# Attention maxima on quarters of the array, in 64-query tiles; score products issued in pairs of heads

## The chip, the cores and the metric

One NeuronCore of one Trainium2 chip runs the whole program. The metric is device time in microseconds. Three runs of the kernel before took 1016.52, 1017.29 and 1020.27 us (median 1017.29). A difference of under 0.5% can't be told from none.

## The reference

Two layers, each a mixer gated by a feed-forward branch, on x of shape (4, 1024, 128). The change touches only the first mixer, causal softmax attention with 16 heads of depth 8:

```python
scores = jnp.einsum('bhnd,bhmd->bhnm', Q, K) / jnp.sqrt(jnp.float32(D_K))
scores = jnp.where(causal[None, None], scores, -jnp.inf)
attn = jax.nn.softmax(scores, axis=-1)
head = jnp.einsum('bhnm,bhmd->bhnd', attn, V)
```

Around it stand a layernorm, rotary embedding, a gelu feed-forward, and in the second layer a retention mixer and a top-2 mixture of eight experts.

## The kernel before, in words

The program runs in stages: projections and first feed-forward, `attention`, the work between the layers, retention with routing, experts. Everything below is in `attention`. Each engine's instruction stream is written out in order; engines meet through semaphores, and no planner reorders anything.

The work is cut into 16 groups (`NQ`), one for each batch and each four heads. Q and K of a group lie in SBUF as `q_groups` and `k_groups`: 64 partitions hold one head (split into bf16 parts, plus two rows that take the negated maximum), so two heads fill the 128 partitions and `hq // 2` selects the pair. A score product of one head uses one 64-row half of TensorE.

Per group there are two streams of 40 items each.

- **Maxima** (`for_maximum`, L877): the row maximum of every query. A unit is 128 queries by up to 512 keys of one head, or of two heads of the same half when the width is at most 256. TensorE writes it to one of four banks (`RING` = 4); on the diagonal two masking matmuls (`causal`, L897) add -1e30 above it. VectorE reduces the bank to one number for each row (`tensor_reduce`, L766). Before unit n is written, `max_read` must say that unit n-4 has been reduced. After the 40 units VectorE combines the two key halves (L769), GpSimd splits the maxima into bf16 parts (L815 to L821), TensorE turns them over (`turn_over`, L874), VectorE copies them out (L756), and SyncE places them by two DMAs in the augmentation rows of Q (`place`, L677).
- **Products** (`for_products`, L906): scores again, now transposed and with the maximum subtracted. A step is 128 keys by up to 512 queries of one head (or two). It goes to one of three banks (`BANKS` = 3); masking matmuls stand at L928. ScalarE takes the exponential into `probs` (L854). Before step n is written, `exp_done` must say that step n-3 is through ScalarE. Five steps behind, `products` (L959) multiplies the probabilities with V in fp32, for four heads at once on tiles of 128 rows by 32 columns. ScalarE copies the finished halves out (`keep`, L841), once after step 4 and once after step 16 of a group, in line with its exponentials.

The loop over group x runs the products of x and, beside them, the maxima of x+1 (units 16 to 39) and x+2 (units 0 to 15). `side_by_side` (L936) issues one product step and one maximum unit on opposite halves of the array, then the masks of both; `turn_over` comes at step 28. `packs`, `units` and `steps` (L595 to L607) are ordered so that both items of a pair have the same width. A prologue does the maxima of group 0 and a part of group 1 before any product.

Of the kernel before, what the change touches and what calls it, by code (L numbers as in the profile page):

```python
# [20 lines left out]
BF16 = mybir.dt.bfloat16  # L21
# [27 lines left out]
ROW = D + 2  # L49
BUFS = 3  # L50
MASKED = -1.0e30
MAGNITUDE = 0x7FFFFFFF
LN_EPS, RMS_EPS, TOP_EPS = 1e-5, 1e-6, 1e-9

# [39 lines left out]
class Groups:  # L94


    def __init__(self, m):
        self.q, self.k = m.sb("q_groups", [P, QUADS, 2, S], BF16), m.sb("k_groups", [P, QUADS, 2, S], BF16)
        self.zeroed = m.sem("groups_zeroed")
        self.loaded = [m.sem(f"groups_loaded{s}") for s in range(QUADS)]  # L100
        self.masks = [m.sb(n, [P, 2, P], BF16) for n in ("chooseB", "hideB", "hide_laterB")]
        self.masks_loaded = m.sem("masks_loaded")

    def load_masks(self, sp, A):
# [484 lines left out]
def attention(nc, A, groups, second, kept_until):  # L589

    NQ = B * QUADS
    slots = [(0, 0), (0, 1), (0, 3), (0, 2), (1, 0), (1, 2), (1, 4), (1, 5), (1, 3), (1, 7), (1, 6), (1, 1)]
    tiles = [(2, 0), (4, 0), (0, 0), (1, 0), (5, 0), (3, 0), (6, 1), (4, 1), (5, 1), (6, 0), (7, 0), (7, 1)]

    def packs(w):  # L595

        return [(0, 2), (1, 3)] if 2 * w <= HALF else [(hq,) for hq in range(4)]

    def max_width(t, c):
        return min(HALF, P * (t + 1) - HALF * c)  # L600

    def slot_width(j):
        c, jt = slots[j]
        return HALF * (c + 1) - max(HALF * c, P * jt)

    units = [(tuple(hq ^ 1 for hq in heads), t, c) for t, c in tiles for heads in packs(max_width(t, c))]
    steps = [(j, heads) for j in range(len(slots)) for heads in packs(slot_width(j))]  # L607
    assert [max_width(t, c) for _, t, c in units[16:] + units[:16]] == [slot_width(j) for j, _ in steps]
# [17 lines left out]
    def offset(heads, hq, w):  # L626

        return heads.index(hq) * w
# [6 lines left out]
    with Space(nc) as m:  # L635
# [6 lines left out]


        q, k, in_loaded = groups.q, groups.k, groups.loaded
        mx, mx2 = m.sb("mxB", [P, 2, 2, 2, NT]), m.sb("mx2B", [P, 2, 2, 2, NT // 2])
# [12 lines left out]
        LOADS, PLACED, STORED, SOURCES = 16 * 5, 16 * 2, HEAD_STORES, 16 * 4  # L658
# [5 lines left out]
        with nc.Block() as block:  # L664
            @block.sync
            def _(sp):
# [73 lines left out]
            def _(dve):  # L740
# [4 lines left out]
                for n, (x, g) in enumerate(order):  # L745
                    if n == AHEAD:
                        nc.vector.memset(empty[:, :, 0:D + 1], 0.0).then_inc(emptied, 1)
                        nc.vector.memset(empty[:, :, D + 1], float(2 * N)).then_inc(emptied, 1)
                    par = x % 2
                    if (x, g) == (SCALED, None):  # L750
                        reciprocals(0)
                    dve.wait_ge(max_done, n + 1)
                    if g is None:
                        if x >= 2:
                            dve.wait_ge(neg_placed[par], PLACED * (x // 2))
                        nc.vector.tensor_copy(neg[:, par, :], mxb[n % RING][0:64, 0:P]).then_inc(max_read, 1)  # L756
                        continue
                    heads, t, c = units[g]
                    w = max_width(t, c)
                    table, col = (mx, t) if c == 0 else (mx2, t - 4)  # L760
                    if len(heads) == 1:
                        dst, src = table[:, par, heads[0] % 2, heads[0] // 2, col:col + 1], mxb[n % RING][:, 0:w]
                    else:
                        dst = table[:, par, heads[0] % 2, :, col]
                        src = mxb[n % RING][:, 0:2 * w].rearrange("p (a w) -> p a w", w=w)
                    nc.vector.tensor_reduce(dst, src, AX.X, ALU.max).then_inc(max_read, 1)  # L766
                    if g == UNITS - 1:
                        dve.wait_ge(max_read, n + 1)
                        nc.vector.tensor_tensor(mx[:, par, :, :, 4:8], mx[:, par, :, :, 4:8], mx2[:, par, :, :, :],  # L769
                                                ALU.max).then_inc(combined, 1)  # L770

                dve.wait_ge(g2["in_loaded"], SOURCES)
# [28 lines left out]
            def _(pool):  # L801
# [10 lines left out]
                def split_maxima(x):  # L812
                    par, upper, lower = x % 2, parts[:, x % 2, 0, :], parts[:, x % 2, 1, :]
                    pool.wait_ge(combined, x + 1)
                    nc.gpsimd.tensor_scalar(lower, mx[:, par, :, :, :].rearrange("p a b t -> p (a b t)"), -1.0, None,  # L815
                                            ALU.mult).then_inc(split, 1)
# [50 lines left out]
            def _(pe):  # L867
# [9 lines left out]
                def for_maximum(x, g):  # L877

                    n = place_of[x, g]
                    s = x % QUADS  # L880
                    heads, t, c = units[g]
                    w = max_width(t, c)
# [4 lines left out]
                    bank = mxb[n % RING]  # L887

                    def score(i):
                        hq = heads[i]  # L890
                        r, to = hq % 2, offset(heads, hq, w)
                        ins = nc.tensor.matmul(bank[:, to:to + w], q[half[r], s, hq // 2, t * P:t * P + P],  # L892
                                               k[half[r], s, hq // 2, HALF * c:HALF * c + w], start=True, stop=(c < t // 4))
                        if c < t // 4:
                            ins.then_inc(max_done, 1)

                    def causal(i, part):  # L897
                        r, to = heads[i] % 2, offset(heads, heads[i], w) + w
                        ins = nc.tensor.matmul(bank[:, to - P + ROWS * part:to], choose[half[r], part, :],  # L899
                                               hide[half[r], part, ROWS * part:P], start=False, stop=(part == 1))  # L900
                        if part == 1 and i == len(heads) - 1:
                            ins.then_inc(max_done, 1)

                    return len(heads), score, None if c < t // 4 else causal

                def for_products(x, e):  # L906

# [79 lines left out]
                for x, g in prologue:  # L987
                    if g is None:
                        turn_over(x)
                    else:  # L990
                        side_by_side(for_maximum(x, g))
                waiting = []
                for x in range(NQ):
                    todo = stream(x)
                    pe.wait_ge(neg_placed[x % 2], PLACED * (x // 2 + 1))
                    for e, (j, heads) in enumerate(steps):
                        both = [for_products(x, e)]
                        if todo and todo[0][1] is None:
                            turn_over(todo.pop(0)[0])
                        if todo:  # L1000
                            both.append(for_maximum(*todo.pop(0)))
                        side_by_side(*both)
                        if e == last_step[j]:
                            waiting.append((x, j))
                        if waiting and due(*waiting[0]) <= UNITS * x + e:
# [1215 lines left out]
def constants():  # L2221
# [22 lines left out]
    hide = np.where(p[None, None, :] > row, MASKED, 0.0)  # L2244
# [72 lines left out]
```

## Time and profile before

| | us |
|---|---|
| Median of three runs | 1017.29 |
| Span of the profiled execution (first to last instruction) | 1008.0 |
| Outside the span, against the median | 9.3 |
| Maxima prologue, then the attention loop | about 117 to 148, then 148 to 540 |
| VectorE busy in a steady stretch of the loop, 215.0 to 482.7 | 254.24 of 267.70 |
| TensorE busy in it (ends are modelled) | 252.06 |
| ScalarE busy in it | 226.13 |

The profile is of one execution. "PE" is TensorE's matmuls, "PEld" its weight loads, "DVE" VectorE, "ACT" ScalarE, "POOL" GpSimd, "SP" SyncE, and a "q" behind a name is that engine's queue, as it issues DMAs. Of the tile in `64*128` the first number is rows of the array, the second columns. Durations of TensorE, VectorE and ScalarE instructions overlap with their successors, so a rate is read from starts, not from durations: of a merged line of n equal instructions it is (length less one duration) over n-1.

### The profile page before, as it was taken

Reading aid. Unit: us, or ns where it says so; the run is one execution under the profiler, and the core shown is the slowest. Engines: PE = TensorE matmul, PEld = TensorE weight load, DVE = VectorE, ACT = ScalarE, POOL = GpSimd, SP = SyncE. Lnnn points to the kernel's source line nnn. Section 1 sums busy time; section 2 is a strip of 40 time slices with the busy share of each in tenths; the row PEclk is TensorE's granted clock in tenths of the full one; section 3 lists DMA queues with packets and bytes.
Section 4 is the critical chain, followed back from the end, with each engine's and each line's share of the span. In section 5 each row is a group of like instructions: output and inputs, shape, how many; then the busy total and the mean of one; then the engine's idle time right before and its main releaser. Section 6 shows DMA issues by size and latency. Waiting matters only on the chain. (4 is left out here: it accounts for less than half of the span.)

```text
span 1008.0 us, 25094 instructions
## 1 busy us (share of the span) xinstructions
PE 874.2 (87%) x9373; PEld 464.7 (46%) x9374; DVE 816.2 (81%) x1699; ACT 725.7 (72%) x1493; POOL 289.1 (29%) x331
## 2 busy tenths in 40 slices
PE   4999899899999999999898898778999999979960
PEld 3666543334333333333344666533444444458850
DVE  6665499899999999999923766589999999928895
ACT  2666408788888888888784454478999999948851
POOL 4865311111111000000003656500344443005560
PEclk9999859999999999999999888768999999989995
DMA  5579851644445353330004899695354643546637
GB/s 167 223 267 331 280 133 42 205 101 105 110 98 125 89 123 84 68 69 14 13 24 127 277 317 301 226 241 101 67 118 94 114 89 54 136 142 189 206 119 252
DMA packets 121560, 147.20 MB, mean 146 GB/s; under 512 B 19213, under 2 KB 81242, under 8 KB 120800
## 3 DMA queue, kind: packets, MB, share of 16 engines
q1 hardware_dynamic: 116064, 133.74, 48.0%
q0 software_dynamic: 5376, 11.85, 4.1%
q8 instruction: 76, 1.25, 0.5%
q14 instruction: 44, 0.36, 0.1%
HBM read 77.63 MB, written 69.54 MB: 146 GB/s over the span
## 5 line engine op out<-in xcount | busy, mean ns | idle before, releaser
L854 ACT ACTIVATE probsB<-psB 128x512 f32<-128x512 f32 (+2 forms) x640 | 310.0, 566 | 87.1 <-PE psB L928 61.5
L766 DVE TENSOR_REDUCE mxB<-psB 128x1 f32<-128x512 f32 (+2 forms) x448 | 256.9, 642 | 11.1 <-PE psB L892 8.3
L921 PE MATMUL psB<-q_groups,k_groups 64*128 64x512 bf16 (+3 forms) x768 | 205.8, 330 | 16.6 <-DVE mxB L766 8.3
L892 PE MATMUL psB<-k_groups,q_groups 64*128 64x512 bf16 (+3 forms) x768 | 217.0, 344 | 2.8 <-PEq L293 1.7
L959 PE MATMUL psB<-probsB,vB 128*32 128x512 f32 (+3 forms) x1536 | 164.5, 500 | 0.7 <-ACT probsB L854 0.5
L1725 ACT ACTIVATE psD<-psD 128x896 f32<-128x896 f32 (+2 forms) x192 | 153.4, 799 | 12.9 <-PE psD L1779 12.7
L921 PEld LDWEIGHTS psB<-q_groups,k_groups 64*128 64x128 bf16 x768 | 67.5, 94 | 161.2 <-ACT probsB L854 140.3
L1656 DVE TENSOR_REDUCE sumsD<-psD 128x1 f32<-128x128 f32 (+3 forms) x256 | 113.2, 481 | 11.8 <-PE psD L1802 9.4
L899 PE MATMUL psB<-hideB,chooseB 64*128 64x128 bf16 (+1 forms) x1024 | 115.1, 210 | 0.0
L1779 PE MATMUL psD<-k_groups,q_groups 64*128 64x512 bf16 (+3 forms) x384 | 104.4, 343 | 12.3 <-ACT psD L1725 5.6
L766 DVE TENSOR_REDUCE mx2B<-psB 128x1 f32<-128x384 f32 (+2 forms) x192 | 104.4, 594 | 8.5 <-PE psB L899 6.9
L928 PE MATMUL psB<-hide_laterB,chooseB 64*128 64x64 bf16 (+1 forms) x1024 | 109.7, 205 | 0.0
L815 POOL TENSOR_SCALAR partsB<-mxB 128x32 f32<-128x32 f32 x16 | 4.6, 290 | 346.7 <-DVE mxB L769 346.7
L928 PEld LDWEIGHTS psB<-hide_laterB,chooseB 64*128 64x128 bf16 x1024 | 88.6, 95 | 19.8 <-issue 1.4
L899 PEld LDWEIGHTS psB<-hideB,chooseB 64*128 64x128 bf16 x1024 | 92.2, 98 | 9.9 <-issue 3.9
L1711 POOL DMA_INDIRECT slot_x<-xD,indexR x64 | 64.4, 1006 | 77.8 <-DVE sumsD L1656 39.5
L1667 DVE TENSOR_TENSOR keptD<-psD,causalD 128x512 f32<-128x512 f32 x128 | 82.5, 680 | 0.3 <-PE psD L1798 0.2
L892 PEld LDWEIGHTS psB<-k_groups,q_groups 64*128 64x128 bf16 x768 | 69.0, 95 | 13.4 <-DVE mxB L766 9.2
L1960 POOL DMA_INDIRECT back<-zE,toE x40 | 44.3, 1107 | 86.8 <-DVE zE L2147 76.7
L1779 PEld LDWEIGHTS psD<-k_groups,q_groups 64*128 64x128 bf16 x384 | 29.8, 96 | 80.8 <-ACT psD L1725 47.4
L1802 PE MATMUL psD<-k_groups,q_groups 64*128 64x128 bf16 (+3 forms) x256 | 64.8, 314 | 0.9 <-DVE keptD L1667 0.9
L1798 PE MATMUL psD<-q_groups,k_groups 64*128 64x128 bf16 x512 | 49.0, 225 | 6.8 <-DVE sumsD L1656 6.2
(227 smaller groups left out, 1504.5 us busy)
## 6 DMA issues: line engine op xcount, KB each, us to landing
v<-vaugA SPq DMA_DIRECT2D x4, 2048.0 KB, 8.9
vB<-v SPq DMA_DIRECT2D x16, 512.0 KB
q_groups<-q SPq DMA_DIRECT2D x32, 200.0 KB
k_groups<-k SPq DMA_DIRECT2D x32, 200.0 KB
q_groups<-q SPq DMA_DIRECT2D x32, 192.0 KB
k_groups<-k SPq DMA_DIRECT2D x32, 192.0 KB
back<-emptyB POOLq DMA_DIRECT2D x16, 256.0 KB, 3.8
o<-outB SPq DMA_DIRECT2D x128, 32.0 KB, 1.8
```

The source lines that it names most:

```text
L766: nc.vector.tensor_reduce(dst, src, AX.X, ALU.max).then_inc(max_read, 1)
L854: nc.scalar.activation(probs[:, n % DEEP, 0:w], st[n % BANKS][:, 0:w], ACT.Exp, scale=DH ** -0.5).then_inc(exp_done, 1)
L892: ins = nc.tensor.matmul(bank[:, to:to + w], q[half[r], s, hq // 2, t * P:t * P + P], k[half[r], s, hq // 2, HALF * c:HALF * c + w], start ...
L899: ins = nc.tensor.matmul(bank[:, to - P + ROWS * part:to], choose[half[r], part, :], hide[half[r], part, ROWS * part:P], start=False, stop ...
L921: ins = nc.tensor.matmul(bank[:, to:to + w], k[half[r], s, hq // 2, jt * P:jt * P + P], q[half[r], s, hq // 2, i0:i0 + w], start=True, sto ...
L928: ins = nc.tensor.matmul(bank[:, to:to + ROWS * (part + 1)], choose[half[r], part, :], hide_later[half[r], part, 0:ROWS * (part + 1)], sta ...
L959: ins = nc.tensor.matmul(pv[VW * hq:VW * hq + VW, HALF - w:HALF], v[:, s, jt, VW * hq:VW * hq + VW], probs[:, (UNITS * x + at) % DEEP, to: ...
L1656: ins = V.tensor_reduce(sums[:, s, unit:unit + 1], src[:, at:at + P * t], AX.X, ALU.add, apply_absolute_value=True)
L1667: V.tensor_tensor(dst[:, :, :, half, :], piece_bank[n % PIECE_RING].rearrange("p (t a i) -> p t a i", t=2, a=2), causal[:, None, None, :]. ...
L1725: nc.scalar.activation(src, src, ACT.Abs, accum_out=sums[:, s, unit:unit + 1]).then_inc(score_read, 1)
L1779: ins = nc.tensor.matmul(score[n % SCORE_RING][:, cols], q[r, s, hq // 2, P * t:P * t + P], k[r, s, hq // 2, cols], start=True, stop=True)
L1802: ins = nc.tensor.matmul(bank[:, at:at + P * t], q[r, s, hq // 2, P * t:P * t + P], k[r, s, hq // 2, 0:P * t], start=True, stop=True)
```

## The change

- Queries of the maxima go in tiles of 64 (`ROW_TILE`). A unit is now (f, t, c): the two heads 2f and 2f+1, query tile t of 16, key half c (None: tile t with keys of half 0 and tile t+8 with half 1, side by side in one bank). Each head writes 64 partitions of the bank, so each score matmul uses a quarter of the array (64 rows by 64 columns), and the units f = 0 and f = 1 use the four different quarters. Widths end at the diagonal in steps of 64. There are still 40 units.
- One masking matmul of 64 columns for each head and diagonal tile, instead of two of 64 and 128 columns.
- The loop issues two product steps side by side (on the two halves), then two maxima units together (`maxima`), every second step, instead of one product step beside one maxima unit each step. `turn_over` stands between the two.
- The maxima lie in another order in `neg`, so `place` issues eight DMAs of one destination row for each group instead of two.

```diff
-    tiles = [(2, 0), (4, 0), (0, 0), (1, 0), (5, 0), (3, 0), (6, 1), (4, 1), (5, 1), (6, 0), (7, 0), (7, 1)]
+    kinds = [(5, 0), (13, 1), (14, 0), (2, None), (1, None), (15, 0), (7, 0), (15, 1), (8, 0), (9, 0), (4, 0), (12, 1), (0, None),
+             (3, None), (10, 0), (6, 0), (11, 0), (14, 1), (12, 0), (13, 0)]
+    def max_width(f, t, c):
+        return min(HALF, first_row(f, t) + ROW_TILE - HALF * c)
+    def heads_of(f, r):
+        return [(2 * f + r, 64 * (r ^ f))] if ROW_TILE == 64 else [(2 * a + r, 64 * (r ^ f) + ROW_TILE * a) for a in range(2)]
+    units = [(f, t, c) for t, c in kinds for f in range(2)]
...
                     for part in range(2):
-                        sp.dma_start(q[AUG + part:AUG + part + ROWS + 1:ROWS, x % QUADS, :, :],
-                                     neg[32 * part:32 * part + 32, x % 2, :]).then_inc(neg_placed[x % 2], 16)
+                        for f in range(2):
+                            for r in range(2):
...
+                                    sp.dma_start(dst, neg[src, x % 2, at:at + ROW_TILE]).then_inc(neg_placed[x % 2], 16)
...
                     def score(i):
+                        ti, ci = segments[i]
+                        w = max_width(f, ti, ci)
+                        last = first_row(f, ti) // HALF > ci
+                        for r in range(2):
+                            for hq, at in heads_of(f, r):
+                                ins = nc.tensor.matmul(bank[at:at + ROW_TILE, w * i:w * i + w],
+                                                       q[half[r], s, hq // 2, first_row(f, ti):first_row(f, ti) + ROW_TILE],
+                                                       k[half[r], s, hq // 2, HALF * ci:HALF * ci + w], start=True, stop=last)
...
+                    def causal(i):
+                        ti, ci = segments[i]
+                        to = max_width(f, ti, ci) * (i + 1)
+                        for r in range(2):
+                            at = 64 * (r ^ f)
+                            ins = nc.tensor.matmul(bank[at:at + 64, to - ROW_TILE:to], choose[half[r], 0, 0:64], hide[half[r], :],
+                                                   start=False, stop=True)
...
+                def maxima(*both):
+                    for i in range(both[0][0]):
+                        for n, score, _ in both:
+                            if i < n:
+                                score(i)
+                        for n, _, causal in both:
+                            if causal and i < n:
+                                causal(i)
...
                     for e, (j, heads) in enumerate(steps):
-                        both = [for_products(x, e)]
-                        if todo and todo[0][1] is None:
-                            turn_over(todo.pop(0)[0])
-                        if todo:
-                            both.append(for_maximum(*todo.pop(0)))
-                        side_by_side(*both)
+                        if e % 2 == 0:
+                            side_by_side(for_products(x, e), for_products(x, e + 1))
+                            if todo and todo[0][1] is None:
+                                turn_over(todo.pop(0)[0])
+                            if todo:
+                                maxima(*[for_maximum(*todo.pop(0)) for _ in range(2)])
```

## Rows read from the trace of the kernel before

**Rows 1.** The page, part 1: busy us (share of the span) x instructions.
```profile
PE 874.2 (87%) x9373; PEld 464.7 (46%) x9374; DVE 816.2 (81%) x1699; ACT 725.7 (72%) x1493; POOL 289.1 (29%) x331
```

**Rows 2.** Busy time by stretch: length, then PE, PEld, DVE, ACT, POOL; granted clock.
```profile
115.00:142.00 27.00, 23.67 (x133) 11.01 (x131) 24.66 (x48) 3.83 (x4) 1.24 (x7) 0.56 0.72 183
...
215.00:482.70 267.70, 252.06 (x3615) 102.68 (x3615) 254.24 (x474) 226.13 (x471) 21.36 (x59) 1.00 0.38 87
...
507.00:535.00 28.00, 26.01 (x269) 11.91 (x265) 6.91 (x29) 23.23 (x51) 1.87 (x2) 1.00 0.32 79
```

**Rows 3.** Waits, 215.0 to 482.7: us in total, times, longest.
```profile
PEld psB L921 <- ACT probsB L854: 101.3, 158, 0.9
...
DVE mxB L766 <- PE psB L892: 6.9, 11, 0.6
```

**Rows 4.** VectorE in order of time: start, length of the merged run, idle before.
```profile
140.60 1.94 DVE L766 TENSOR_REDUCE mxB<-psB 128x1 f32<-128x384 f32 x4
...
262.70 0.27 DVE L756 CAST negB<-psB 64x128 bf16<-64x128 f32 x1
...
264.25 8.53 DVE L766 TENSOR_REDUCE mxB<-psB 128x1 f32<-128x512 f32 x15 [0.63 <-PE psB L892]
...
277.02 4.86 DVE L766 TENSOR_REDUCE mxB<-psB 128x1 f32<-128x512 f32 x8
...
286.55 0.27 DVE L756 CAST negB<-psB 64x128 bf16<-64x128 f32 x1
```

**Rows 5.** TensorE's matmuls in order of time, five short stretches.
```profile
264.24 0.38 PE L892 MATMUL psB<-k_groups,q_groups 64*128 64x512 bf16 x1
264.55 0.85 PE L959 MATMUL psB<-probsB,vB 128*32 128x384 f32 x8
265.33 0.23 PE L921 MATMUL psB<-q_groups,k_groups 64*128 64x128 bf16 x1
...
265.48 0.22 PE L921 MATMUL psB<-q_groups,k_groups 64*128 64x128 bf16 x1
...
270.18 0.39 PE L921 MATMUL psB<-q_groups,k_groups 64*128 64x512 bf16 x1
...
270.49 0.38 PE L892 MATMUL psB<-k_groups,q_groups 64*128 64x512 bf16 x1
...
271.64 0.19 PE L899 MATMUL psB<-hideB,chooseB 64*128 64x64 bf16 x1
271.75 1.06 PE L959 MATMUL psB<-probsB,vB 128*32 128x512 f32 x8
272.75 0.33 PE L921 MATMUL psB<-q_groups,k_groups 64*128 64x384 bf16 x1
...
273.01 0.32 PE L892 MATMUL psB<-k_groups,q_groups 64*128 64x384 bf16 x1
...
301.48 0.43 PE L959 MATMUL psB<-probsB,vB 128*32 128x128 f32 x8
...
301.84 0.39 PE L921 MATMUL psB<-q_groups,k_groups 64*128 64x512 bf16 x1
```

**Rows 6.** One loop of TensorE, ScalarE and weight load, in order of time.
```profile
267.53 0.60 ACT L854 ACTIVATE probsB<-psB 128x512 f32<-128x512 f32 x1
...
268.02 0.39 PE L921 MATMUL psB<-q_groups,k_groups 64*128 64x512 bf16 x1
...
268.51 2.06 ACT L854 ACTIVATE probsB<-psB 128x512 f32<-128x512 f32 x4 [0.37 <-PE psB L921]
...
270.18 0.09 PEld L921 LDWEIGHTS psB<-q_groups,k_groups 64*128 64x128 bf16 x1 [0.41 <-ACT probsB L854]
```

**Rows 7.** Placing the maxima; last row: DMA issues, with us to landing.
```profile
197.66 0.39 PE L921 MATMUL psB<-q_groups,k_groups 64*128 64x512 bf16 x1 [1.65 <-DMA q_groups<-negB]
...
286.85 1.08 SPq L677 DMA_DIRECT2D q_groups<-negB  x2
...
o<-outB SPq DMA_DIRECT2D x116, 32.0 KB, 2.1
```

More of the change, by code:

```diff
@@ L51 @@
 MASKED = -1.0e30
+ROW_TILE = 64
 MAGNITUDE = 0x7FFFFFFF
@@ L100, in __init__ @@
         self.loaded = [m.sem(f"groups_loaded{s}") for s in range(QUADS)]
-        self.masks = [m.sb(n, [P, 2, P], BF16) for n in ("chooseB", "hideB", "hide_laterB")]
+        self.masks = [m.sb(n, shape, BF16) for n, shape in (("chooseB", [P, 2, P]), ("hideB", [P, ROW_TILE]), ("hide_laterB", [P, 2, P]))]
         self.masks_loaded = m.sem("masks_loaded")
@@ L592, in attention @@
     slots = [(0, 0), (0, 1), (0, 3), (0, 2), (1, 0), (1, 2), (1, 4), (1, 5), (1, 3), (1, 7), (1, 6), (1, 1)]
-    tiles = [(2, 0), (4, 0), (0, 0), (1, 0), (5, 0), (3, 0), (6, 1), (4, 1), (5, 1), (6, 0), (7, 0), (7, 1)]
[L595 to L600, printed above, removed]
+    kinds = [(5, 0), (13, 1), (14, 0), (2, None), (1, None), (15, 0), (7, 0), (15, 1), (8, 0), (9, 0), (4, 0), (12, 1), (0, None),
+             (3, None), (10, 0), (6, 0), (11, 0), (14, 1), (12, 0), (13, 0)]
     def slot_width(j):
@@ L604, in slot_width, with packs, row_tile, first_row @@
         return HALF * (c + 1) - max(HALF * c, P * jt)
-    units = [(tuple(hq ^ 1 for hq in heads), t, c) for t, c in tiles for heads in packs(max_width(t, c))]
+    def packs(w):
+        return [(0, 2), (1, 3)] if 2 * w <= HALF else [(hq,) for hq in range(4)]
+    def row_tile(f, t):
+        return 16 * f + t if ROW_TILE == 64 else 2 * t + f
+    def first_row(f, t):
+        return ROW_TILE * (t if ROW_TILE == 64 else 2 * t + f)
+    def max_width(f, t, c):
+        return min(HALF, first_row(f, t) + ROW_TILE - HALF * c)
+    def heads_of(f, r):
+        return [(2 * f + r, 64 * (r ^ f))] if ROW_TILE == 64 else [(2 * a + r, 64 * (r ^ f) + ROW_TILE * a) for a in range(2)]
+    def parts_of(f, t, c):
+        return [(t, 0), (t + 8, 1)] if c is None else [(t, c)]
+    units = [(f, t, c) for t, c in kinds for f in range(2)]
     steps = [(j, heads) for j in range(len(slots)) for heads in packs(slot_width(j))]
-    assert [max_width(t, c) for _, t, c in units[16:] + units[:16]] == [slot_width(j) for j, _ in steps]
+    assert len(units) == len(steps)
     UNITS, SLOTS_B = len(units), len(slots)
@@ L644, in attention @@
         q, k, in_loaded = groups.q, groups.k, groups.loaded
-        mx, mx2 = m.sb("mxB", [P, 2, 2, 2, NT]), m.sb("mx2B", [P, 2, 2, 2, NT // 2])
+        mx = m.sb("mxB", [P, 2, 2, 2, 16])
         neg = m.sb("negB", [64, 2, P], BF16)
@@ L657, in attention @@
         neg_placed = [m.sem(f"neg_placedB{p}") for p in range(2)]
-        LOADS, PLACED, STORED, SOURCES = 16 * 5, 16 * 2, HEAD_STORES, 16 * 4
+        LOADS, PLACED, STORED, SOURCES = 16 * 5, 16 * 8 * (64 // ROW_TILE), HEAD_STORES, 16 * 4
         SCALED, PROJECT_AT, TURN_AT = QUADS + 3, 2, 20
@@ L676, in place @@
                     for part in range(2):
-                        sp.dma_start(q[AUG + part:AUG + part + ROWS + 1:ROWS, x % QUADS, :, :],
-                                     neg[32 * part:32 * part + 32, x % 2, :]).then_inc(neg_placed[x % 2], 16)
+                        for f in range(2):
+                            for r in range(2):
+                                row, src = ROWS * r + AUG + part, slice(32 * part + 16 * f, 32 * part + 16 * f + 16)
+                                for hq, at in heads_of(f, r):
+                                    dst = q[row:row + 1, x % QUADS, hq // 2, :]
+                                    dst = dst.rearrange("p (t i) -> p t i", i=ROW_TILE) if ROW_TILE == 64 else (
+                                        dst.rearrange("p (t f i) -> p f t i", f=2, i=ROW_TILE)[:, f])
+                                    sp.dma_start(dst, neg[src, x % 2, at:at + ROW_TILE]).then_inc(neg_placed[x % 2], 16)
                 def store(x, c):
@@ L757, in _ @@
                         continue
[L758 to L762, printed above, removed]
-                    else:
-                        dst = table[:, par, heads[0] % 2, :, col]
-                        src = mxb[n % RING][:, 0:2 * w].rearrange("p (a w) -> p a w", w=w)
+                    f, t, c = units[g]
+                    w = max_width(f, t, c or 0)
+                    if c is None:
+                        dst, src = mx[:, par, :, f, t], mxb[n % RING][:, 0:2 * w].rearrange("p (a w) -> p a w", w=w)
+                    else:
+                        dst, src = mx[:, par, c, f, t - 8 * c:t - 8 * c + 1], mxb[n % RING][:, 0:w]
                     nc.vector.tensor_reduce(dst, src, AX.X, ALU.max).then_inc(max_read, 1)
@@ L814, in split_maxima @@
                     pool.wait_ge(combined, x + 1)
-                    nc.gpsimd.tensor_scalar(lower, mx[:, par, :, :, :].rearrange("p a b t -> p (a b t)"), -1.0, None,
+                    nc.gpsimd.tensor_scalar(lower, mx[:, par, 0, :, :].rearrange("p f t -> p (f t)"), -1.0, None,
                                             ALU.mult).then_inc(split, 1)
@@ L880, in for_maximum @@
                     s = x % QUADS
-                    heads, t, c = units[g]
-                    w = max_width(t, c)
+                    f, t, c = units[g]
                     if n >= RING:
@@ L886, in for_maximum @@
                         pe.wait_ge(in_loaded[s], LOADS * (x // QUADS + 1))
-                    bank = mxb[n % RING]
+                    bank, segments = mxb[n % RING], parts_of(f, t, c)
                     def score(i):
[L890 to L894, printed above, removed]
-                            ins.then_inc(max_done, 1)
@@ L897, in causal @@
[L897 to L901, printed above, removed]
+                        ti, ci = segments[i]
+                        w = max_width(f, ti, ci)
@@ new lines, in score @@
+                        last = first_row(f, ti) // HALF > ci
+                        for r in range(2):
+                            for hq, at in heads_of(f, r):
+                                ins = nc.tensor.matmul(bank[at:at + ROW_TILE, w * i:w * i + w],
+                                                       q[half[r], s, hq // 2, first_row(f, ti):first_row(f, ti) + ROW_TILE],
+                                                       k[half[r], s, hq // 2, HALF * ci:HALF * ci + w], start=True, stop=last)
@@ new lines, in score @@
+                        if last:
+                            ins.then_inc(max_done, 1)
+                    def causal(i):
[5 more added lines that the diff above has]
+                                                   start=False, stop=True)
+                        if i == len(segments) - 1:
@@ L902, in causal @@
                             ins.then_inc(max_done, 1)
-                    return len(heads), score, None if c < t // 4 else causal
+                    on_diagonal = first_row(f, t) // HALF == (c or 0)
+                    return len(segments), score, causal if on_diagonal else None
                 def for_products(x, e):
@@ L990, in _ @@
                     else:
-                        side_by_side(for_maximum(x, g))
+                        maxima(for_maximum(x, g))
                 waiting = []
@@ L2243, in constants @@
     choose = np.where(p[None, None, :] == row, 1.0, 0.0)
-    hide = np.where(p[None, None, :] > row, MASKED, 0.0)
+    hide = np.where(np.arange(ROW_TILE)[None, :] > p[:, None] % ROW_TILE, MASKED, 0.0)
     hide_later = np.where(p[None, None, :] < row, MASKED, 0.0)
```

2 lines of the change are left out of this document (1 added, 1 removed).

## The prediction

> **What bounds the kernel now.** I read the page's busy shares first [rows 1]: TensorE is busy 87% of the span, VectorE 81%, ScalarE 72%, which says little, as the stages have different limits. So I took busy time by stretch next. In the steady attention loop [rows 2] VectorE is busy 254.24 of 267.70 us (95%), TensorE 252.06 with modelled ends, ScalarE 226.13. The waits of that stretch [rows 3] decide between the first two: VectorE's longest account with TensorE is 6.9 us, 11 times, while TensorE's loads for a product wait for ScalarE 158 times. VectorE in order of time [rows 4] shows reductions back to back and one 0.63 us hole behind each turn-over. One group takes 286.55 - 262.70 = 23.85 us, cast to cast. VectorE is the bound; TensorE follows it through the ring of four banks.
>
> VectorE's rate, from starts [rows 4]: 512 columns (4.86 - 0.68) / 7 = 0.598 us, 384 columns (1.94 - 0.55) / 3 = 0.464. That is 1.05 ns a column and 0.06 us an instruction. The 40 units of a group hold 18,432 columns: 19.3 + 2.5 us, with cast and combine 22.1, and 1.7 us idle make the 23.85.
>
> TensorE's prices [rows 5] (w columns at the granted 1.00, 2.4 GHz, stream in w / 2.4 ns: 0.213 us for 512):
> - a score pair with its masks: 512 wide 270.49 - 270.18 = 0.31; 384 wide 273.01 - 272.75 = 0.26; packed 128, 265.48 - 265.33 = 0.15 for each of two; packed 256 by the same slope 0.20. Masks alone are about 0.09.
> - a change of tile shape: from the last score of 512 at 264.24 to the probabilities-times-V matmuls (PV below) at 264.55 is 0.31, less 0.213 streaming: 0.09. From a 64-column mask at 271.64 to 271.75 is 0.11, less 0.03: 0.09 again.
> - PV with the change back: 512 wide 272.75 - 271.75 = 1.00, 384 wide 0.78, 128 wide 0.36, 256 between them 0.57. Less 0.09 each: 0.91, 0.69, 0.27, 0.48.
>
> A group has 18,432 columns of score pairs (7.68), 32 masked pairs (2.7), 12 PV (six of 512, two each of 384, 256, 128: 8.3), 24 changes of shape (2.2) and the turn-over (0.3): 21.2 us of TensorE, under VectorE's 22.1.
>
> **What the change does to each engine.**
>
> *VectorE.* Widths end at multiples of 64: the 20 kinds sum to 8,704, twice that is 17,408 columns, still 40 reductions. Saved: 1,024 x 1.05 ns = 1.07 us a group. This is a gain only if VectorE stays the bound.
>
> *TensorE, work.* Product scores pairwise: 4 masked pairs of 512 (0.31), 8 unmasked (0.21), 4 masked of 384 (0.26), 2 packed of 128 (twice 0.14) and 2 of 256 (twice 0.205) are 5.4 us a group. Maxima: if four quarters stream at once, 8,704 columns / 2.4 = 3.6 us, with 16 rounds of 64-column masks, each about 0.06 with its load (between the 0.03 of streaming and the 0.09 of today's masks): 4.6. The bounds are 4.6 and, if only two stream at once, 8.2. I take 4.6, since PV already runs four matmuls on four column strips together: two passes of 512 columns for four heads, eight matmuls, end in 1.06 us [rows 5]. PV 8.3, turn-over 0.3. Scores are thus 10.0 instead of 10.4: pairing saves almost nothing, because before the pair was product and maximum.
>
> *TensorE, changes of shape.* The order is now products (64*128), maxima (64*64), products again, or PV (128*32) between. That is 2 x 20 + 12 = 52 changes a group instead of 24. The trace shows no change between 64*128 and 64*64; the bounds are 0 and the 0.09 of the nearest rows (rows 5). I take 0.09, for both changes that can be read have it: 4.7 us. Sum of the work: 5.4 + 4.6 + 8.3 + 4.7 + 0.3 = 23.3 us, above VectorE's new 21.0.
> The Trainium skill, TensorEngine Tiling (Array Packing), section Key Properties, says that changing the tiling mode drains the TensorEngine, while changing only the tile does not. The trace agrees for the changes it has, 0.09 us each; no row shows whether 64*64 beside 64*128 counts as another mode. By the rule the forecast stands, without it the first rival below.
>
> *TensorE, the new wait.* There are three score banks. A pair (e, e+1) may be written only when the exponential of e-2 is done, which is the *first* of the pair before. So from one pair to the next lies at least: score to ScalarE's start 268.51 - 268.02 = 0.49 [rows 6], one exponential 0.60, wake-up about 0.07 (four exponentials take 2.06, so they start 0.487 apart, and the third ends at 268.51 + 0.97 + 0.60 = 270.08; the load that waits for it starts at 270.18; 0.07 is an estimate below this 0.10). That is 1.15 us for 512 unmasked, 1.24 masked, 1.09 for 384 masked, 0.99 and 1.34 for the packed ones of 128 and 256. Before, the wait reached three single steps back and bound nothing. Behind the waiting instruction stand the maxima units, so VectorE is starved by it too, and PV, since TensorE runs in order.
> PV stands in every second pair of a single-head slot. The pair with PV costs its work: 512 masked 0.31 + 0.09 + 0.21 + 0.09 + 0.91 + 0.09 = 1.70. The one without has 0.7 of work but may not follow sooner than 1.24. Two pairs: 2.94 (unmasked 2.75), where VectorE needs 4 x 0.598 = 2.39.
>
> *The group.* Pair by pair, the larger of work and wait (pair number = step / 2): 1.27, 1.24, 1.63, 1.81, 0.99, 1.34, 1.39, 1.15, then 2.94 for pairs 8 and 9, 1.70, 1.24, 1.66, 1.09, 1.91 (turn-over), 1.45, 0.99, 1.34, 1.67, 1.15. Pair 3 holds 0.18 because its PV waits for ScalarE's copy of the group before; pairs 8 and 9 because the exponential of step 18 stands behind the copy after step 16, which waits for PV of pair 8. Sum 27.96: 23.3 of work and 4.7 of waits. Against 23.85: +4.1 us a group, for the 14 groups that run both streams: +57.5.
>
> *The rest.* The last but one group loses its maxima half way (27 us before; estimate +1). The last has products alone [rows 2]: pairs now share the array, but the wait of about 1.15 a pair makes 24 us of 20 pairs, and it took about 26 with the output projection in it: 0, bounds -3 and +2. The prologue is VectorE's (24.66 busy of 27): 1,280 columns less, -1.3.
>
> *Placing.* Eight DMAs at 0.54 us to issue [rows 7] are 4.3 us where two took 1.1. The first goes out 0.30 behind the cast (286.55 to 286.85), the last 3.8 later, and it lands between 2.1 (the nearest store) and some 4 us after that: 6 to 8 us from the cast. The pairs behind the cast now last about 8, so it hides mostly, but not in the prologue nor in the group at 197.66, which already waits 1.65 for it: +3 in all, bounds +1 and +12 (0.8 a group).
>
> **Sum.** 57.5 + 1 + 0 - 1.3 + 3 = +60. The span goes from 1008.0 to 1068, and with the 9.3 us around it from 1017.3 to 1077.
>
> **The rivals.**
> - *No cost between 64*128 and 64*64.* 0.09 less in the ten pairs that are bound by work: 0.85 x 14 = 12 less, 1065. For: only the column split changes. Against: both changes seen cost the same.
> - *Quarters in one bank take turns.* The two heads of a unit lie in different row halves but in one bank. Then the maxima stream twice as long: +2.4 us a group in the work-bound pairs, +34, 1111. For: today's two halves always write to different banks, so the trace shows nothing that excludes it. Against: the partitions differ. The Trainium skill, same page, section Gotcha 1: PSUM Pressure, says that different row tiles can't access the same PSUM bank at once; no row here shows it.
> - *The other side: VectorE stays the bound.* If two pairs take TensorE under 2.39 us, VectorE goes on back to back and only its saving counts: 1.07 x 14 + 1.3 = 16 less, 1001. It is one mechanism, the in-order chain of scores, maxima and PV hiding in VectorE's ring of four, and it decides at 2.39. For: VectorE has two units in hand while TensorE does PV. Against: PV with its changes (1.0), two shared score rounds (0.5) and one wait (1.15) already exceed it with free changes of shape.
> - *It evens out.* Waits overlap with work so far that a group takes its 23.9 us; 1017.
>
> **Chances.** Forecast 0.63 (1077, own range 1062 to 1092), free change of shape 0.12 (1065), turns in a bank 0.12 (1111), VectorE stays 0.08 (1001), even 0.05. The range of 1045 to 1112 leaves out the last two and tails. Faster by over 0.5% 0.08, within 0.5% (what a measurement here can't tell from none) 0.05, slower 0.87.
>
> **What would show it.** In the loop: cast to cast about 28 us; VectorE busy near 21 of 28 with waits for TensorE in every second pair; the load of each product pair waiting for ScalarE; 0.09 beyond streaming from the last product score to the first maximum; four maxima matmuls starting within 0.03. Cast to cast under 23.85, or VectorE above 90% busy, would make the prediction wrong, and first of all the bank wait.

## The result, and the profile after

The changed kernel takes 1097.72 us (median of 4 runs, 1095.68 to 1098.78) against 1016.9 (4 runs) before: ratio 1.0784, interval 1.0755 to 1.0813. I had forecast 1077. The profiled execution spans 1097.0 us, from the first instruction to the last. Every run lies about 1.8 us above the span of its core, so the 9.3 us that I put outside the span before were mostly one quick execution: its 1008.0 us of span stand for about 1010 of time. The ratios below are of fast executions alone; the one slow execution, of e4 at 1896 us, is left out.

The page, part 1, and busy time by stretch (length, then PE, PEld, DVE, ACT, POOL), the steady loop and the last group, against [rows 1, 2]. L949 are now the score matmuls of the products, L956 their masks, L915 and L926 those of the maxima, L997 the products with V, L875 the exponentials, L787 the reductions.

```profile
PE 900.6 (82%) x10142; PEld 465.3 (42%) x10142; DVE 814.7 (74%) x1699; ACT 737.9 (67%) x1493; POOL 289.3 (26%) x331
```
```profile
215.00:475.00 260.00, 218.26 (x3303) 83.39 (x3306) 203.51 (x378) 187.98 (x377) 20.25 (x51) 1.00 0.36 82
...
591.00:619.00 28.00, 20.52 (x234) 8.92 (x234) 6.91 (x29) 21.16 (x43) 1.87 (x2) 1.00 0.40 100
```

No engine is near full in the loop: VectorE fell from 95% to 78%, TensorE is at 84% and ScalarE at 72%. VectorE in order of time has the casts of two groups [rows 4] 28.95 us apart, and between them ten holes of 0.38 to 0.97 us, two of which are here:

```profile
288.53 0.28 DVE L779 CAST negB<-psB 64x128 bf16<-64x128 f32 x1
...
311.80 1.29 DVE L787 TENSOR_REDUCE mxB<-psB 128x1 f32<-128x512 f32 x2 [0.78 <-PE psB L915]
313.54 1.29 DVE L787 TENSOR_REDUCE mxB<-psB 128x1 f32<-128x512 f32 x2 [0.46 <-PE psB L915]
...
317.48 0.28 DVE L779 CAST negB<-psB 64x128 bf16<-64x128 f32 x1
```

The waits of 220.0 to 500.0 (total us, times, longest), against [rows 3]:

```profile
PEld psB L949 <- ACT probsB L875: 127.5, 183, 1.4
ACT probsB L875 <- PE psB L956: 44.1, 105, 1.1
...
DVE mxB L787 <- PE psB L926: 39.3, 65, 1.0
ACT probsB L875 <- PE psB L949: 20.4, 40, 0.8
DVE mxB L787 <- PE psB L915: 18.2, 32, 0.8
```

VectorE waits for TensorE 57.5 us in 97 waits; ScalarE and TensorE wait for each other. A pair is steps 2p and 2p + 1 of a group. TensorE in order of time through pairs 11 and 12 shows why:

```profile
342.03 0.39 PE L949 MATMUL psB<-q_groups,k_groups 64*128 64x512 bf16 x2
342.25 0.25 PE L956 MATMUL psB<-hide_laterB,chooseB 64*128 64x64 bf16 x4
342.43 0.41 PE L915 MATMUL psB<-k_groups,q_groups 64*64 64x512 bf16 x4
343.34 0.34 PE L949 MATMUL psB<-q_groups,k_groups 64*128 64x384 bf16 x2 [0.49 <-ACT probsB L875]
...
343.69 0.36 PE L915 MATMUL psB<-k_groups,q_groups 64*64 64x384 bf16 x4
343.88 0.20 PE L926 MATMUL psB<-hideB,chooseB 64*64 64x64 bf16 x4
344.01 1.06 PE L997 MATMUL psB<-probsB,vB 128*32 128x512 f32 x8
345.00 0.34 PE L949 MATMUL psB<-q_groups,k_groups 64*128 64x384 bf16 x2
```

And ScalarE beside it, with the idle time before each run:

```profile
342.60 1.08 ACT L875 ACTIVATE probsB<-psB 128x512 f32<-128x512 f32 x2 [0.67 <-PE psB L956]
343.84 0.87 ACT L875 ACTIVATE probsB<-psB 128x384 f32<-128x384 f32 x2 [0.16 <-PE psB L956]
```

ScalarE starts on the pair of 342.03 at 342.60, its first exponential ends 0.60 later, and the next pair starts at 343.34: 1.31 us, in which TensorE has 0.75 of work (what the same pair takes in e1 below). Then everything behind that wait, products, maxima and PV (the block of probabilities times V), takes 345.00 - 343.34 = 1.66. Four steps cost 2.98 us (2.97 by the rounded starts). Before they cost 2.52, by the starts of the same steps in TensorE's order of time, pair 11 at 306.25, pair 12 at 307.15 and the next at 308.76:

```profile
306.25 0.38 PE L921 MATMUL psB<-q_groups,k_groups 64*128 64x512 bf16 x1
...
307.15 0.33 PE L921 MATMUL psB<-q_groups,k_groups 64*128 64x384 bf16 x1
...
307.50 1.06 PE L959 MATMUL psB<-probsB,vB 128*32 128x512 f32 x8
...
308.76 0.32 PE L921 MATMUL psB<-q_groups,k_groups 64*128 64x384 bf16 x1
```

Where 81 us went, by starts of the first exponential: 14 full groups +71.6, the last but one +4.8, the last +3.0; the first product starts 2.7 later (150.7 against 148.0). That is 82. The two profiled spans differ by 89.0; the other 7 lie behind the attention, in work that the change doesn't touch, and that took between 467 and 481 us in the fourteen profiles.

### The profile page after: what moved, and what is told of

It reads as the page before. It is cut to its first block and busy times, and to the rows that moved or that the text cites. A ratio compares the mean times of both kernels' runs of the same rounds, so it can differ in the third digit from the quotient of the medians.

```text
span 1097.0 us, 26753 instructions
## 1 busy us (share of the span) xinstructions
PE 900.6 (82%) x10142; PEld 465.3 (42%) x10142; DVE 814.7 (74%) x1699; ACT 737.9 (67%) x1493; POOL 289.3 (26%) x331
## 5 line engine op out<-in xcount | busy, mean ns | idle before, releaser
L787 DVE TENSOR_REDUCE mxB<-psB 128x1 f32<-128x512 f32 (+7 forms) x640 | 354.8, 605 | 96.8 <-PE psB L926 63.8
L875 ACT ACTIVATE probsB<-psB 128x512 f32<-128x512 f32 (+2 forms) x640 | 320.4, 554 | 141.8 <-PE psB L956 104.0
L949 PE MATMUL psB<-q_groups,k_groups 64*128 64x512 bf16 (+3 forms) x768 | 125.4, 332 | 77.6 <-ACT probsB L875 70.4
L997 PE MATMUL psB<-probsB,vB 128*32 128x512 f32 (+3 forms) x1536 | 166.4, 506 | 3.0 <-ACT outB L862 2.6
L915 PE MATMUL psB<-k_groups,q_groups 64*64 64x512 bf16 (+7 forms) x1536 | 136.7, 346 | 5.4 <-DVE mxB L787 2.6
L949 PEld LDWEIGHTS psB<-q_groups,k_groups 64*128 64x128 bf16 x768 | 42.3, 93 | 226.3 <-ACT probsB L875 212.8
L915 PEld LDWEIGHTS psB<-k_groups,q_groups 64*64 64x64 bf16 x1536 | 46.7, 106 | 58.4 <-DVE mxB L787 33.4
L956 PE MATMUL psB<-hide_laterB,chooseB 64*128 64x64 bf16 (+1 forms) x1024 | 60.6, 204 | 0.0
L956 PEld LDWEIGHTS psB<-hide_laterB,chooseB 64*128 64x128 bf16 x1024 | 49.7, 95 | 11.4 <-issue 0.7
L926 PE MATMUL psB<-hideB,chooseB 64*64 64x64 bf16 x1024 | 50.5, 195 | 0.0
L2076 ACT ACTIVATE hTE<-psE,b1E 128x320 f32<-128x320 f32 x64 | 33.3, 527 | 24.1 <-PE psE L2035 23.5
L997 PEld LDWEIGHTS psB<-probsB,vB 128*32 128x32 f32 x1536 | 30.8, 108 | 41.4 <-issue 35.4
```

Of the source, the lines that this page charges most:

```text
L875: nc.scalar.activation(probs[:, n % DEEP, 0:w], st[n % BANKS][:, 0:w], ACT.Exp, scale=DH ** -0.5).then_inc(exp_done, 1)
L915: ins = nc.tensor.matmul(bank[at:at + ROW_TILE, w * i:w * i + w], q[half[r], s, hq // 2, first_row(f, ti):first_row(f, ti) + ROW_TILE], k[ ...
L949: ins = nc.tensor.matmul(bank[:, to:to + w], k[half[r], s, hq // 2, jt * P:jt * P + P], q[half[r], s, hq // 2, i0:i0 + w], start=True, sto ...
L956: ins = nc.tensor.matmul(bank[:, to:to + ROWS * (part + 1)], choose[half[r], part, :], hide_later[half[r], part, 0:ROWS * (part + 1)], sta ...
L997: ins = nc.tensor.matmul(pv[VW * hq:VW * hq + VW, HALF - w:HALF], v[:, s, jt, VW * hq:VW * hq + VW], probs[:, (UNITS * x + at) % DEEP, to: ...
```

## The experiments

All twelve ran beside the kernel before; ratios are to it, as it ran beside them (its medians were 1012.9 us for e1 to e4, 1018.1 for e5 to e8 and 1017.2 for e9 to e12). "Group" is the steady time of a group. Pairs 11 and 12 are start to start of the product pairs, the second with a PV block of 512 columns.

| kernel | ratio (interval) | group | pair 11 | pair 12 | both |
|---|---|---|---|---|---|
| before | 1 | 23.85 | 0.91 | 1.61 | 2.52 |
| changed | 1.078 (1.076 to 1.081) | 28.94 | 1.31 | 1.67 | 2.98 |
| e1 waits split | 1.062 (1.057 to 1.068) | 27.94 | 0.75 | 2.13 | 2.88 |
| e2 old maxima, in pairs | 1.065 (1.060 to 1.071) | 28.20 | 1.31 | 1.60 | 2.91 |
| e3 e2, waits split | 1.048 (1.041 to 1.054) | 27.19 | 0.61 | 2.20 | 2.81 |
| e4 four score banks | 1.063 (1.055 to 1.070) | 28.36 | 0.75 | 2.25 | 3.00 |
| e5 maxima first | 1.062 (1.057 to 1.067) | 27.84 | 1.31 | 1.35 | 2.66 |
| e6 e5, waits split | 1.047 (1.043 to 1.050) | 26.81 | 0.94 | 1.63 | 2.57 |
| e7 single products | 1.051 (1.047 to 1.055) | 27.07 | 1.21 | 1.67 | 2.88 |
| e8 before, four score banks | 1.013 (1.009 to 1.017) | 24.75 | 1.02 | 1.61 | 2.63 |
| e9 half exponentials | 1.053 (1.049 to 1.056) | 26.90 | 1.10 | 1.67 | 2.76 |
| e10 before, half exponentials | 0.994 (0.991 to 0.996) | 23.35 | 0.69 | 1.61 | 2.30 |

**The loop through ScalarE, shortened (e9, e10).** This is the most direct test. From group 3 on each exponential covers half the columns of its step, so part of the softmax is left out; TensorE's and VectorE's instructions stay the same.

```diff
-                        w = slot_width(j) * len(heads)
+                        w = slot_width(j) * len(heads) // (2 if x > 2 else 1)
```

> The changed kernel with the exponentials of groups 3 to 15 on half the columns of a step (the other half of the probabilities keeps older values): part of the softmax is left out, TensorE's and VectorE's instructions are the same. ScalarE takes about 0.33 us for a step instead of 0.60. Theory (the loop score, exponential, freed bank sets the distance of two pairs): every pair without a long PV block comes 0.27 us sooner, down to its work, and pairs 3 and 9 lose their copy chain: 2.7 us less a group, 26.3 (25.8 to 26.8), ratio to the kernel before 1.047 (1.04 to 1.055). Rival (TensorE's matmuls and changes of shape fill the time): a group within 0.3 us of 28.9.

TensorE and ScalarE of e9 in order of time, at the same pair:

```profile
334.80 0.39 PE L949 MATMUL psB<-q_groups,k_groups 64*128 64x512 bf16 x2
335.20 0.41 PE L915 MATMUL psB<-k_groups,q_groups 64*64 64x512 bf16 x4
335.90 0.34 PE L949 MATMUL psB<-q_groups,k_groups 64*128 64x384 bf16 x2 [0.28 <-ACT probsB L875]
```
```profile
335.37 0.66 ACT L875 ACTIVATE probsB<-psB 128x256 f32<-128x256 f32 x2 [1.10 <-PE psB L956]
```

The distance fell from 1.31 to 1.10, as the exponential fell from 0.60 to 0.38; it is still 0.57 from matmul to ScalarE's start. Pairs 0, 2, 10, 12, 14, 15 and 18, which are bound by work, did not change by 0.01 us; pairs 1, 4, 5, 7, 11, 13, 16, 17 and 19 each lost 0.11 to 0.21, and pair 9 lost 0.42. The group is 26.90, just above the 25.8 to 26.8 that was forecast (the saving is 0.22 a pair, not 0.27, and pair 3 kept its chain through the copy); the ratio, 1.053, is inside its range. The rival is out: the same matmuls and changes of shape took 2.0 us less.

> The same omission in the kernel before. Theory: VectorE bounds it, with ScalarE's loop just under it, so a group goes from 23.85 to no less than 23.0, ratio 0.99 (0.985 to 1.0). Rival (the kernel before is held by the same loop): 22 us or less a group, ratio under 0.98.

23.35: the theory held. The kernel before has a little of the same loop, since it gained 0.5 us (pair 11 went from 0.91 to 0.69).

**Each wait just before its own matmul (e1).**

```diff
-                    if n >= BANKS:
-                        pe.wait_ge(exp_done, n - BANKS + 1)
                     bank = st[n % BANKS]
                     def score(i):
+                        if i == 0 and n >= BANKS:
+                            pe.wait_ge(exp_done, n - BANKS + 1)
```

> The changed kernel, but each of the two product steps of a pair waits for its own score bank just before its first matmul, instead of both waits before either matmul. The first of a pair then goes out one exponential earlier and ScalarE has it in hand. My theory (the bank wait is what holds the pairs without a probabilities-times-V block at about 1.3 us): those pairs drop to their work, a group from 28.94 to 24.0 to 25.0 us, the whole to about 1030 us (1020 to 1042). Rival (TensorE's work, with its changes of tile shape and its quarters, is the cost): a group stays above 28 us, the whole within 1% of 1098 us.

A miss for both: 27.94. TensorE of e1 in order of time, and its weight loads with the wait inside the pair:

```profile
336.19 0.39 PE L949 MATMUL psB<-q_groups,k_groups 64*128 64x512 bf16 x2
...
336.94 0.81 PE L949 MATMUL psB<-q_groups,k_groups 64*128 64x384 bf16 x2
...
337.76 0.36 PE L915 MATMUL psB<-k_groups,q_groups 64*64 64x384 bf16 x4
...
338.07 1.06 PE L997 MATMUL psB<-probsB,vB 128*32 128x512 f32 x8
339.07 0.34 PE L949 MATMUL psB<-q_groups,k_groups 64*128 64x384 bf16 x2
```
```profile
337.41 0.09 PEld L949 LDWEIGHTS psB<-q_groups,k_groups 64*128 64x128 bf16 x1 [0.38 <-ACT probsB L875]
```

The pair without PV indeed fell to its work, 0.75. But the fourth product step since PV (337.41) still waits for the exponential of the first (from 336.19: 1.22 us), and the maxima and PV stand behind it: 1.66 to the next pair. Three banks allow three steps ahead, whatever the form of the wait. So the price of four steps is first product to freed bank, plus all that is issued in order behind that wait. My forecast had taken the wait for the pair's own.

**The old maxima in the new order (e2), and with split waits (e3).**

```diff
+                        if e % 2 == 0:
+                            side_by_side(for_products(x, e), for_products(x, e + 1))
...
+                            if todo:
+                                side_by_side(*[for_maximum(*todo.pop(0)) for _ in range(2)])
```

> The kernel before (maxima of 128 queries on 64x128 tiles, two placing DMAs), with only the order changed: two product steps side by side, then two maxima units side by side. My theory (bank wait first, change of tile shape second): a group 27.8 to 28.4 us, 0.1 us less in the ten pairs bound by work, the whole about 1084 us (1076 to 1092). Rival (the 28 added changes of shape are the main cost): 28.94 - 2.7 = 26.2 us, about 1057 us. Rival (the quarters are the main cost): back to 23.9 us, about 1017 us.

28.20, as forecast: with no quarters, no added changes of shape and two placing DMAs, the order alone costs 4.35 of the 5.1 us. Both rivals are out. TensorE of e2 in order of time at pair 11:

```profile
334.71 0.39 PE L921 MATMUL psB<-q_groups,k_groups 64*128 64x512 bf16 x2
334.94 0.25 PE L928 MATMUL psB<-hide_laterB,chooseB 64*128 64x64 bf16 x4
335.03 0.38 PE L892 MATMUL psB<-k_groups,q_groups 64*128 64x512 bf16 x2
335.24 0.25 PE L899 MATMUL psB<-hideB,chooseB 64*128 64x128 bf16 x4
336.02 0.34 PE L921 MATMUL psB<-q_groups,k_groups 64*128 64x384 bf16 x2 [0.53 <-ACT probsB L854]
```

> As the one before, with the waits of a product pair taken one at a time. TensorE's work is then 21.4 us a group by the sum of the prediction, below VectorE's 22.1. My theory: VectorE is the bound again, a group 23.3 to 24.6 us, the whole about 1017 us (1010 to 1030). Rival (the order in pairs costs in itself, whatever the waits): above 26 us, 1050 us or more.

27.19; my theory missed and the rival held. The reason is the one seen in e1, as far as the pairs tell (0.61 and 2.20): the pair of maxima stands behind the wait in the stream, where in the kernel before one of its two units goes out beside the product.

**Only the place of the maxima (e5, e6).**

```diff
+                            first = bool(waiting) and due(*waiting[0]) <= UNITS * x + e + 1
+                            if not first:
+                                side_by_side(for_products(x, e), for_products(x, e + 1))
...
+                            if first:
+                                side_by_side(for_products(x, e), for_products(x, e + 1))
```

> The changed kernel with one thing in another order: in a pair of steps that ends with a probabilities-times-V block, the two maxima units are issued ahead of the two product steps, so they lie in the time in which TensorE waits for ScalarE. Nothing is added or taken away but some 7 changes of shape. Theory as the first runs leave it: two pairs cost first product to freed bank (1.26 us) plus all that stands behind the wait (products, maxima, PV: 1.7). With the maxima ahead, 1.4 stands behind: 0.3 us less in seven or eight pairs, a group 26.3 to 27.0 us, the ratio to the kernel before 1.045 (1.035 to 1.055). Rival (TensorE's work is the bound, waits only fill it): only the changes of shape count, 0.7 us a group, 28.2 us, ratio 1.068 or more.

27.84, ratio 1.062: a miss for both, less than the theory's gain and more than the rival's. TensorE of e5 in order of time:

```profile
334.02 0.39 PE L949 MATMUL psB<-q_groups,k_groups 64*128 64x512 bf16 x2
334.42 0.57 PE L915 MATMUL psB<-k_groups,q_groups 64*64 64x512 bf16 x8
335.33 0.34 PE L949 MATMUL psB<-q_groups,k_groups 64*128 64x384 bf16 x2 [0.30 <-ACT probsB L875]
335.68 1.07 PE L997 MATMUL psB<-probsB,vB 128*32 128x512 f32 x8
336.68 0.34 PE L949 MATMUL psB<-q_groups,k_groups 64*128 64x384 bf16 x2
...
338.16 0.41 PE L915 MATMUL psB<-k_groups,q_groups 64*64 64x512 bf16 x4 [0.28 <-DVE mxB L787]
```

Where it applies it does what it should: the maxima go into the waiting time, 1.31 + 1.35 = 2.66 for 2.98. But only pairs 3, 9, 10, 12, 14 and 15 gain (0.22 to 0.34 each). The others with a PV block don't: pair 2, for one, is followed by a pair that has a block too, whose maxima now lie ahead of it and so in the place of pair 2's own (1.64 us, as in the change). And pair 13 takes 0.67 longer, since behind the turn-over two pairs of maxima follow each other and the second waits for VectorE (338.16).

> Both edits: maxima ahead of the products before a PV block, and each product's wait just before its own matmul. Theory: the gains of the two add (1.0 for the wait, 2.3 for the order), a group 25.3 to 26.2 us, ratio 1.03 (1.02 to 1.045). Rival (both act on the same idle time): no better than the order alone, 26.3 us or more.

26.81, ratio 1.047: the theory's 25.3 to 26.2 missed, because the order alone gained only 1.1. The rival's number holds, but not the rival, which had both acting on the same idle time and so no gain over the order alone: 1.00 for the wait and 1.10 for the order are 2.10, and 2.13 was measured. It has the shortest group of the versions with quarters, and is far from the kernel before.

**The quarters alone (e7).**

```diff
-                            side_by_side(for_products(x, e), for_products(x, e + 1))
+                            side_by_side(for_products(x, e))
...
+                        else:
+                            side_by_side(for_products(x, e))
```

> The quarters alone: two maxima units together every second step as in the change, but the product steps go out one at a time, one ahead of the maxima and one behind, each with the wait of the kernel before (three steps back). Theory: a masked slot costs 0.31, 0.1, 0.21, 0.1, 0.31 shared with the next step, 0.1, 0.21, 0.1, then 0.31 and PV 1.1: 2.86 us for four steps against 3.0 in the change and 2.6 before; a group 27.0 to 28.5 us, ratio 1.05 to 1.07. So pairing the products gains nothing and the maxima block in the in-order stream is the cost. Rival (pairing the products with its double wait is the whole cost): near the kernel before, under 25 us, ratio 1.02 or less.

27.07, and 2.88 for the four steps: as forecast. Issued in blocks, quarters cost 3.2 us a group with no pairing of products at all. So the pairing is the smaller part: taking it out gives back 1.9 of the 5.1 us.

**Banks moved from maxima to scores (e4, e8).**

```diff
-    RING, BANKS = 4, 3
+    RING, BANKS = 3, 4
```

> The changed kernel with four banks for scores and three for maxima instead of three and four. A product pair then waits for nothing in practice, but a maxima pair may be written only when the first unit of the pair before has been reduced: 0.50 to VectorE's start, 0.68 for a reduction, 0.07 to wake, 1.25 us, so the wait moves from ScalarE's exponentials to VectorE's reductions. My theory: a group 28.0 to 29.5 us, the whole 1085 to 1105 us, and the waits of TensorE for ScalarE turn into waits for VectorE. Rival (only the score banks matter): a group 24 to 25 us, about 1030 us.

28.36 a group, as forecast. The whole, 1076.58 us, is below the 1085 to 1105 forecast: the last two groups take 28.2 and 24.4 where the change has 32.2 and 28.6, and the kernel before beside it took 1012.86. TensorE of e4 in order of time, now held by VectorE in the middle of the pair:

```profile
338.15 0.34 PE L949 MATMUL psB<-q_groups,k_groups 64*128 64x384 bf16 x2
339.09 0.36 PE L915 MATMUL psB<-k_groups,q_groups 64*64 64x384 bf16 x4 [0.52 <-DVE mxB L787]
```

> The kernel before with four banks for scores and three for maxima. Theory: VectorE is its bound and holds only two finished units over a PV block of 1.1 us instead of three, so it runs dry: a group 24.5 to 26.5 us against 23.85, ratio 1.01 to 1.04. Rival (the wait of products for ScalarE is what costs the kernel before its 1.7 us idle a group): faster, 22.5 to 23.5 us, ratio 0.98 to 0.995.

24.75, as forecast: the split of banks in the kernel before was the better one.

**The hole behind the turn-over in the kernel before (e11, e12).** Since VectorE is its bound, I tried to close the hole of [rows 4]; e11 is the first edit, e12 both.

```diff
-    AHEAD, DELAY = 16, 4
+    AHEAD, DELAY = 16, 6
...
-                        both = [for_products(x, e)]
                         if todo and todo[0][1] is None:
                             turn_over(todo.pop(0)[0])
+                        both = [for_products(x, e)]
```

> The kernel before with the turn-over two steps later (step 30 instead of 28), so that a PV block of 512 columns doesn't follow it at once. VectorE's idle 0.63 us behind each turn-over should go: 23.3 us a group, ratio 0.991 (0.987 to 0.997). Rival (VectorE's hole only moves to the next PV block): 23.85, ratio 1.0.

> As the one before, and the turn-over is issued ahead of the wait of its step for ScalarE, in which TensorE is idle about 0.5 us. If the hole is TensorE's lateness, another 0.1 to 0.2 us a group: 23.1 to 23.3, ratio 0.988 to 0.995. If it isn't, the same as the one before within 0.002.

VectorE of e11 in order of time:

```profile
262.49 0.69 DVE L766 TENSOR_REDUCE mxB<-psB 128x1 f32<-128x512 f32 x1 [0.27 <-PE psB L892]
263.09 0.27 DVE L756 CAST negB<-psB 64x128 bf16<-64x128 f32 x1
263.29 8.04 DVE L766 TENSOR_REDUCE mxB<-psB 128x1 f32<-128x512 f32 x14
```

The hole shrank from 0.63 to 0.27 and moved ahead of the cast; a group takes 23.59 (e11) and 23.57 (e12) instead of 23.85, between what the theory and the rival of e11 said. The ratios are 0.998 (0.996 to 1.000) and 0.999 (0.997 to 1.001): no difference that these runs can tell from none, so e11's 0.991 missed, and issuing the turn-over ahead of the wait added nothing that can be told. Nothing that I ran and that does all of the work is shown to be faster than the kernel before.

## Why the prediction was right, point by point

- *The size.* 1097.7 us lies outside the 1062 to 1092 that I gave this mechanism. It is inside the whole range only because that reached to 1112 for the rival of turns in a bank, which is out; so much of the hit is luck. The direction and the mechanism were forecast, 60 of the 81 us with them.
- *VectorE bounds the kernel before; its saving counts only while it does.* Right. VectorE's columns did fall, but it is idle for 56 of 260 us, and the saving doesn't show in its busy time either: 22.7 us a group before and after (254.24 of 267.70, 203.51 of 260.00). A pair of reductions alone shows 1.29 us where the rate in a row gives 1.20.
- *The bank wait.* Right in place, short in size: I took 0.07 us to wake TensorE, below the 0.10 of my own row, and 1.24 for a masked pair; it is 1.31 (0.57 to ScalarE, 0.60, and 0.14 to the matmul). Over pairs 1, 3, 4, 5, 7, 11, 13, 16, 17 and 19, with 0.09 in each of the packed ones 4 and 16, this is 0.65 of the 0.98 us by which a group was longer than the 27.96 forecast. Pairs 8 and 9, forecast as one sum of 2.94, took 3.08; each other pair came within 0.09 us of its forecast.
- *What the wait is.* My text had it as the pair's own. e1 and e3 show that it belongs to the three banks between two PV blocks, and e5 that its cost is what stands in order behind it. The sum for the change was the same either way; the forecasts for e1 and e3 failed by it.
- *Changes of shape.* About 0.10 us from 64*128 to 64*64. After the same masked product pair the maxima start 0.40 us later in the change (342.03 to 342.43) and 0.32 in e2 (334.71 to 335.03), where they have the products' shape. e2 as a whole is 0.74 us a group faster, though with wider reductions and fewer placing DMAs too. The rival without this cost is out. The Trainium skill (TensorEngine Tiling (Array Packing), Key Properties) says that a change of mode drains the engine; this agrees, though only the column split changed.
- *Quarters in one bank take turns.* Out. The four matmuls of 384 columns start at 343.69 and the masks behind them at 343.88: 0.19 us, where streaming 384 columns once is 0.16 and twice 0.32. PV starts at 344.01, 0.32 after the first of them, with masks and a change of shape between. The four are two pairs, and the two of a pair share a bank from different row halves. The Trainium skill (same page, Gotcha 1: PSUM Pressure) says that different row tiles can't access one bank at once; for different partitions of it, the measurement says otherwise.
- *VectorE stays the bound.* Out: two pairs take 2.98, over the 2.39 where it decides.
- *The rest.* The last but one group cost +4.8, not +1, a slip of mine: its first twelve pairs, which run as in any group, are 2.9 longer by their exponentials. The last cost +3.0, outside my bounds of -3 to +2. The first product came 2.7 later, where -1.3 and a part of the +3 for placing were forecast (the cast ahead of it came at 142.59 and 142.46, so no saving in the prologue can be read); in the loop, placing showed in three waits, 2.3 us in all between 215 and 485. The forecast fell 21 us short: 14 of it in the 14 groups (0.98 each), the rest here.

## What to carry to other kernels

With n banks between an in-order producer and a consumer, count from the longest block in the producer's stream: n steps go out behind it, the next waits for the consumer's answer to the first of them, and the cycle costs that round trip plus all that is issued behind the wait. With three banks here that was the fourth step (e1). Batching work of one kind moves more of the stream behind the wait, even if the batch itself runs faster: the maxima in quarters and in pairs left a group of 28.94 us for 23.85. Before a second engine's instructions are made cheaper, see whether the order that makes them cheap leaves that engine the bound.

## What was not expected of the hardware

SyncE took 5.63 us to issue the eight placing DMAs, 0.70 each, against 0.54 for each of the two larger ones before [rows 7]. Over the thirteen such lines up to 500 us it is 4.94 to 6.64 us, 0.62 to 0.83 each. Why a smaller one takes longer isn't shown. The line of one group:

```profile
347.83 5.63 SPq L701 DMA_DIRECT2D q_groups<-negB  x8
```
